# Moving the second half's gate matmuls, its sums and the finish of a graph in a two-layer graph kernel

## The reference

```python
h = relu(layernorm(x))
# layer 0: a convolution branch, a message branch and a gated update
x_conv = relu(bn(conv17(relu(bn(conv1(h))))) + h)
dist   = sq[:, None] + sq[None, :] - 2 * s @ s.T          # s = h @ w_se.T + b_se
A      = exp(-dist) * adj
x_nmp  = A @ relu(h @ w_msg.T + b_msg)
gi = concat(x_conv, x_nmp) @ w_ih.T + b_ih                # parts r, z, n
gh = h @ w_hh.T + b_hh
r, z = sigmoid(gi_r + gh_r), sigmoid(gi_z + gh_z)
x1 = x + (1 - z) * tanh(gi_n + r * gh_n) + z * h
# layer 1
h2  = relu(layernorm(x1))
out = x1 + relu(h2 @ W[:256] + (adj @ h2) @ W[256:] + bias)
```

## Time and profile before

| what | value |
| --- | --- |
| median of three runs | 1932.36 us |
| the profiled execution's own time | 1935.05 us |
| its span, first to last instruction | 1932.8 us |
| instructions | 36810 |
| TensorE matmuls busy | 1785.4 us, 92% |
| VectorE busy | 1531.6 us, 79% |
| ScalarE busy | 841.0 us, 44% |
| GpSimd busy | 439.1 us, 23% |
| mean granted TensorE clock | 0.982 of full speed |
| `distances` of graph 0 and of graph 63 start at | 625.0 and 1891.4 us |

### The profile page before, as it was taken

One profiled execution on the slowest core, in us unless ns is written; L12 is line 12 of the kernel. 1 busy time (PEld: TensorE's weight loads), 2 busy tenths in 40 slices (PEclk: granted clock), 3 DMA queues, 4 the chain that ended last, 5 costly groups with the idle time before them and its releaser, 6 DMA issues.

```text
span 1932.8 us, 36810 instructions
## 1 busy us (share of the span) xinstructions
PE 1785.4 (92%) x12477; PEld 1167.3 (60%) x12478; DVE 1531.6 (79%) x3386; ACT 841.0 (44%) x1489; POOL 439.1 (23%) x616
## 2 busy tenths in 40 slices
PE   2778999977779999999999999999999999999997
PEld 1566777732334666666666666666666666666664
DVE  4899999944544788888888888888888888888886
ACT  3664544432233444444444444444444444444442
POOL 3521111100001222222222222222222222222221
PEclk9899999998989999999999999999999999999998
DMA  6376676578684223222232222322223222232320
GB/s 190 108 277 231 220 267 201 193 261 278 190 276 138 76 73 100 79 90 90 72 103 77 91 89 72 103 76 94 86 72 106 74 96 84 73 106 72 97 83 17
DMA packets 172018, 245.55 MB, mean 127 GB/s; under 512 B 14428, under 2 KB 110675, under 8 KB 171210
## 3 DMA queue, kind: packets, MB, share of 16 engines
q1 hardware_dynamic: 171960, 244.81, 38.6%
HBM read 154.57 MB, written 90.18 MB: 127 GB/s over the span
## 4 chain that ended last, share of the span: by engine, by line
PE 36%; DVE 23%; ACT 5%; issue 4%; DVEq 1%; POOL 0%; POOLq 0%
PE ps_rz L1557 16%; PE ps_l L1557 12%; PE ps_n L1557 6%; ACT big L1702 2%; ACT big L1597 2%; DVE big L1693 2%; DVE big L1592 2%; DVE big L1627 2%; DVE big L1649 2%; DVE big L1601 2%; DVE big L1584 2%; DVE big L1736 2%; DVE big L1710 1%; PE ps_d L1771 1%; DVE big L1740 1%
## 5 line engine op out<-in xcount | busy, mean ns | idle before, releaser
L1557 PE MATMUL ps_rz<-big 128*128 128x512 f16 x2304 | 561.2, 380 | 12.0 <-DVE big L1649 9.6
L1557 PEld LDWEIGHTS ps_rz<-big 128*128 128x128 f16 x2304 | 220.1, 98 | 223.5 <-DVE big L1649 20.8
L1271 PE MATMUL m_ps<-big 128*128 128x512 f16 (+1 forms) x1152 | 280.9, 384 | 45.4 <-DVE ysb L1034 42.9
L1557 PE MATMUL ps_n<-big 128*128 128x256 f16 x2304 | 314.3, 273 | 0.0
L1557 PEld LDWEIGHTS ps_n<-big 128*128 128x128 f16 x2304 | 225.2, 98 | 94.6
L1557 PE MATMUL ps_l<-big 128*128 128x512 f16 (+1 forms) x1536 | 273.1, 328 | 2.9 <-DVE big L1806 1.5
L1727 POOL TENSOR_TENSOR big<-big 128x256 f32<-128x256 f32 x128 | 97.5, 761 | 671.1 <-ACT big L1720 671.1
L1702 ACT ACTIVATE big<-big,w_scale 128x512 f32<-128x512 f32 x128 | 92.0, 719 | 287.0 <-DVE big L1693 287.0
L1271 PEld LDWEIGHTS m_ps<-big 128*128 128x128 f16 x1152 | 112.2, 100 | 159.7 <-DVE ysb L1034 56.0
L1557 PEld LDWEIGHTS ps_l<-big 128*128 128x128 f16 x1536 | 150.1, 98 | 91.9 <-issue 2.7
L1557 PE MATMUL ps_b<-big 128*128 128x256 f16 x1536 | 190.3, 274 | 1.5 <-DVE big L1627 1.5
(11 more groups left out here) (239 smaller groups left out, 2874.4 us busy)
## 6 DMA issues: line engine op xcount, KB each, us to landing
spectra<-ysb SPq DMA_DIRECT2D x96, 256.0 KB, 2.6
big<-spectra SPq DMA_DIRECT2D x64, 384.0 KB, 3.4
xin<-in_x SPq DMA_DIRECT2D x64, 256.0 KB, 3.2
x_normed<-front SPq DMA_DIRECT2D x64, 256.0 KB, 3.4
h_turned<-front SPq DMA_DIRECT2D x64, 256.0 KB, 2.5
xin<-in_adj SPq DMA_DIRECT2D x64, 256.0 KB, 3.1
big<-h_turned SPq DMA_DIRECT2D x64, 256.0 KB, 3.2
big<-in_adj SPq DMA_DIRECT2D x64, 256.0 KB, 3.6
```

The costliest lines, as they stand in the source:

```text
L1271: last = pe.matmul(dest, x_, w_, start=n == 0, stop=n == 11, skip_group_check=True)
L1557: last = pe.matmul(dest, stationary(dl), moving(wl), start=start and n == 0, stop=stop and n == 2, **kw)
```

## The change

On TensorE, `gates_second` of half 1 goes ahead of `neighbours` of graph t-1. On VectorE, `gate_sums` of half 1 moves from the beginning of the next slot to the end of its own; `weighted_low` goes ahead of `adj_split_low`; and `finish` is cut in two and done a slot later. Its first instruction (L1823, now in `out_row`) is done for graph t-2: half 0 ahead of `weighted_low`, and half 1 behind `adj_split_low`, ahead of `norm2`. The other (L1827) is done for both halves behind `h2_split_low`. SyncE's store is of graph t-2. There is one slot more at the end, and each slot has a new flag `old`. No instruction of computation is added or taken away.

```diff
+        def out_row(dve, t, p, i):
+            ready(dve, "out_done", t, i + 1, H)
+            dve.scalar_tensor_tensor(out=out_sum[:, i, :], in0=ps_l[i][:, 0:D], scalar=w["scale"][:, 11:12],
+                                     in1=w["bias_out"][:, :], op0=ALU.mult,
+                                     op1=ALU.add).then_inc(S["out_added"], 1)
+
         def finish(dve, t, p):
             if not (isinstance(t, int) and t < 2):
 
                 dve.wait_ge(stored[p], (t - p) * 8)
             for i in range(H):
-                ready(dve, "out_done", t, i + 1, H)
-                dve.scalar_tensor_tensor(out=out_sum[:, i, :], in0=ps_l[i][:, 0:D], scalar=w["scale"][:, 11:12],
-                                         in1=w["bias_out"][:, :], op0=ALU.mult,
-                                         op1=ALU.add).then_inc(S["out_added"], 1)
                 ready(dve, "out_added", t, i + 1, H)
...
-            slot(0, 0, False, True, True)
-            slot(1, 1, True, True, True)
+            slot(0, 0, False, False, True, True)
+            slot(1, 1, False, True, True, True)
...
-            slot(graphs, 0, True, False, False)
+            slot(graphs, 0, True, True, False, False)
+            slot(graphs + 1, 1, True, False, False, False)
...
-                    if prev:
-                        store(sp, t - 1, 1 - p)
+                    if old:
+                        store(sp, t - 2, p)
...
                     if prev:
-                        gate_sums(dve, t - 1, 1 - p, 1)
                         gate_new(dve, t - 1, 1 - p, 1)
...
                     if prev:
                         x1_rows(dve, t - 1, 1 - p, 1)
                         x1_stats(dve, t - 1, 1 - p, 1)
+                    if old:
+                        out_row(dve, t - 2, p, 0)
                     if cur:
+                        weighted_low(dve, t, p)
                         adj_split_low(dve, t, p)
-                        weighted_low(dve, t, p)
+                    if old:
+                        out_row(dve, t - 2, p, 1)
                     if prev:
                         norm2(dve, t - 1, 1 - p)
                     if cur:
                         gate_sums(dve, t, p, 0)
                     if prev:
                         h2_split_low(dve, t - 1, 1 - p)
+                    if old:
+                        finish(dve, t - 2, p)
...
                     if nxt:
                         conv_split_low(dve, t + 1, 1 - p)
-                    if prev:
-                        finish(dve, t - 1, 1 - p)
+                    if cur:
+                        gate_sums(dve, t, p, 1)
...
                         first_conv_rz(pe, t, p, 1)
                         first_conv_n(pe, t, p, 1)
+                    if cur:
+                        gates_second(pe, t, p, 1)
                     if prev:
                         neighbours(pe, t - 1, 1 - p)
-                    if cur:
-                        gates_second(pe, t, p, 1)
```

More of the change, by code:

```diff
@@ L1831, in slots @@
         def slots(engine, slot):
-            slot(0, 0, False, True, True)
-            slot(1, 1, True, True, True)
+            slot(0, 0, False, False, True, True)
+            slot(1, 1, False, True, True, True)
             with engine.Fori(1, (graphs - 2) // 2) as j:
                 for p in range(2):
-                    slot(j * 2 + p, p, True, True, True)
-            slot(graphs - 2, 0, True, True, True)
-            slot(graphs - 1, 1, True, True, False)
-            slot(graphs, 0, True, False, False)
+                    slot(j * 2 + p, p, True, True, True, True)
+            slot(graphs - 2, 0, True, True, True, True)
+            slot(graphs - 1, 1, True, True, True, False)
+            slot(graphs, 0, True, True, False, False)
+            slot(graphs + 1, 1, True, False, False, False)
         with nc.Block() as block:
@@ L1844, in _, with slot @@
             def _(sp):
-                def slot(t, p, prev, cur, nxt):
+                def slot(t, p, old, prev, cur, nxt):
                     if nxt:
```

## The result

The changed kernel took 1960.14 us (median of 4 runs, 1955.56 to 1961.23) against 1930.53 (4 runs, 1928.65 to 1933.15): a ratio over the single runs of 1.0148, 95% interval 1.0125 to 1.017 (the two medians alone give 1.0153). It is slower, by 1.5%. 1955 was forecast.

What follows compares the result with a forecast made beforehand. TensorE was taken to set the pace at 20.11 us a slot, only its waits winnable; +24.1 (61 slots of +0.395), -0.5 and -1.2 made +22.4 us, 1955 us from the 1932.36 median, range 1936 to 1976.

Steps and rivals of the forecast that it cites:

- Part 1: `gates_second` ahead of `neighbours`, sums at the slot's end: the wait ahead of `weighted` goes, -0.04 us a slot.
- Part 2: `weighted_low` ahead of `adj_split_low`: L1649 starts about 0.03 us behind L1644, `gates_second` comes 0.17 us earlier.
- W to T: Time from the start of `weighted` to `turn2`: 4.92 us without the meeting, 5.55 with it.
- Part 3: Ahead of `norm2`: the second L1760 meets GpSimd's L1533 and is held; average +0.395 us a slot, with parts 1 and 2.
- rival 1: VectorE gets in first or there is no shutting out at `norm2`: -16.0 us, 1916 us; chance 0.20.
- rival 3: GpSimd wins only about a third of slots, or the meeting costs little: terms cancel, 1932 us; chance 0.04.
- The term that was too small: The average change of a slot, forecast at +0.395 us in 61 slots, +24.1 us.
- the 14.96 from T to the next W: Time in us from `turn2` to the next slot's `weighted`, without waits; everything behind `turn2` was to follow it, change 0.
- The ends: Slots 1 and 63 gain about 0.25 us each, and the finish after the last slot gives -1.2 us.

Runs made afterwards that it cites:

- norm_first: The changed kernel with `norm2` moved ahead of the second `out_row` (half 1); 0.9929 of the kernel before, 1921.25 against 1934.58 us.
- pool_waits: The changed kernel, VectorE's order untouched, with GpSimd's `conv_add` waiting until `norm2` is through; 0.9919 of the kernel before, 1918.3 us.
- waits2: The changed kernel with two already satisfied GpSimd waits ahead of L1533; one run of 1915.63 us, slots of 19.90 us.
- waits3: The changed kernel with three already satisfied GpSimd waits ahead of L1533; one run of 1916.38 us, slots of 19.90 us.
- waits1: The changed kernel with one already satisfied GpSimd wait ahead of L1533; one run of 1939.56 us, slots of 20.28 us.
- all four rebuilt ones: norm_first, pool_waits, swap_only, and the changed kernel with `adj_split_low` back ahead of `weighted_low`; 0.9914 to 0.9929 of the kernel before.
- swap_only: The kernel before with only `weighted_low` put ahead of `adj_split_low`; 0.9926 of the kernel before, 1920.73 us.
- late512: The changed kernel with a 128x512 VectorE memset, into a tile nothing reads, ahead of `norm2`; one run of 1974.79 us, slots of 20.87 us.

## Why the prediction was right

**Part 1** was right. The wait ahead of `weighted` is gone, the sums of half 1 end ahead of the slot's end, and there is no new wait of TensorE for them.

**Part 2** was right. L1649 starts 0.04 behind L1644's end (1308.71 + 0.60, then 1309.35), and in norm_first W to T is 4.93 for the 4.92 that was worked out. Slots of 19.897 for 19.87 make the gain 0.215 for 0.235.

**Part 3** was right in mechanism, place and price. The second L1760 was to start together with L1533 and started 0.01 apart; it was to end 0.15 behind it, and did; W to T was to be 5.55 and is 5.56. pool_waits, waits2 and waits3 show the cause by moving GpSimd alone. But the margin was thinner than the chances said, and that the kernel fell on this side of it was in part luck. The point lies at a lead of 0.06 (waits1), inside the 0.02 to 0.1 of rival 1, and the kernel is at -0.01: with GpSimd 0.09 later (waits2) the same change took 1915.63 us in its one run, against 1934.68 of the kernel before, which is rival 1. The mixture of rival 3, which I called unlikely, is what waits1 does: GpSimd won 32 of 61 slots.

**The term that was too small** is the slot: +0.454 us for +0.395. 0.05 of the difference is behind T. Before, `turn2` to the next group is 0.44 us, and the first of its weight loads begins 0.11 ahead of it (1338.35), while other matmuls still run; once `turn2` waits, that load begins with it, and the group takes 0.49 (1312.68 to 1313.17). The weight loads of `turn2`, before and after:

```profile
1338.24 0.47 PEld L1771 LDWEIGHTS ps_d<-ident,big 128*128 128x128 f32 x4
```

```profile
1312.67 0.42 PEld L1771 LDWEIGHTS ps_d<-ident,big 128*128 128x128 f32 x4 [0.74 <-DVE big L1760]
```

The prediction took the 14.96 from T to the next W over, and that was wrong by 0.05 in each of 61 slots, 3 us.

**The ends** were -2.4 for -1.45 (the -1.7 without slot 1, which lies in the windows). 0.74 of the difference is TensorE's clock in the last `layer1`. It takes 4.56 us instead of 5.30, because the granted clock came back from 1.2 to 2.4 GHz while it ran. Why it came back earlier than before no run shows; TensorE had been idle for 5.25 us ahead of `turn2` here, and for 6.56 in the kernel before. TensorE's timeline of the changed kernel, and the windows of its `layer1` (the clock is the third figure from the right):

```profile
1944.69 1.11 PE L1771 MATMUL ps_d<-ident,big 128*128 128x128 f32 x4 [5.25 <-DVE big L1760]
...
1947.22 4.56 PE L1557 MATMUL ps_l<-big 128*128 128x512 f16 x12 [1.42 <-DVE big L1783]
```

```profile
1948.00:1952.00 4.00, 3.78 (x11) 1.26 (x9) 0.00 (x0) 0.18 (x1) 0.00 (x0) 0.64 0.18 66
```

In the kernel before, `layer1` ran from 1920.70 to 1926.00, and the window of its last 2 us still had 0.52:

```profile
1920.70 5.30 PE L1557 MATMUL ps_l<-big 128*128 128x512 f16 x12 [1.42 <-DVE big L1783]
```

```profile
1924.00:1926.00 2.00, 2.00 (x5) 0.46 (x3) 0.00 (x0) 0.00 (x0) 0.00 (x0) 0.52 0.00 0
```

The sum of the slots and the ends, +28.15 - 2.4, is the +25.7 of the two spans. The medians differ by 29.6, and the ratio of 1.0148 makes +28.6; the first stage, the same in all these kernels, put graph 1's start anywhere between 639 and 649 us in the profiles, so a few us between medians carry no meaning.

The best version by slot length is pool_waits or norm_first, 19.897; by time all four rebuilt ones (0.9914 to 0.9929) can't be told apart. swap_only gets there with two lines exchanged.

## What to carry to other kernels

When an order written out by hand is changed, work out what each moved instruction now runs beside on the engine that can shut it out, not only what it waits for. An addition of 1.16 us on GpSimd, whose delay cost TensorE nothing in pool_waits, made an instruction of 0.41 us on the path take 1.29. Two edits that gain nearly the same 0.2 us each by themselves may collide when made together, so time them apart. If the start of two such instructions comes out within 0.1 us of each other, put one of them clearly behind: in pool_waits one wait for the other instruction, on the engine that has time, was enough.

## What the runs showed of the hardware

- The turn between a VectorE TENSOR_SCALAR with two scalars from pointers and a GpSimd addition is decided at a lead of 0.06 us of the former: it lost with -0.01 in all 61 slots of the changed kernel, lost or won with 0.05 to 0.06 in waits1, and won with 0.08 in all of waits2. The Trainium skill, "SBUF — State Buffer", section "Who interferes with whom", says that issue order decides; the starts in the profile agree with it in the changed kernel and in waits2, but not in waits1, where VectorE lost 32 of 61 slots with a lead of 0.05 to 0.06.
- The one who loses is held until the other is through: the second L1760 ended 0.15 behind L1533's end (changed kernel), and a held L1533 ended 1.02 behind the end of the second L1760 (waits1).
- In late512 L1534 began 0.17 us after a VectorE memset of 0.48 and 0.23 ahead of the first L1761, and still came after that L1761. That the memset kept GpSimd out is what this suggests; it isn't shown by itself.
- The memset of f32 took 218, 272, 325, 378 and 485 ns for 192, 256, 320, 384 and 512 columns: 0.83 ns a column.
- Behind a memset the first of two L1760 took 0.23 us instead of 0.41, and the second started 0.15 behind it instead of 0.32. I have no cause for it.
